# A decoder stack on one core: the order of TensorE's steps in the first cross attention

## The chip, the core and the metric

The kernel runs on one core of a Trainium2 chip. The metric is the device time of one execution in microseconds, in which all six layers of the stack run one after the other.

## What is computed

The reference is two decoder layers on x of 8 batches, 512 tokens and 256 channels. Each layer adds self attention, cross attention over a context of 512 tokens, and a feed forward part. The change touches only the cross attention of the first layer:

```
q = x_q @ W_q;  kv = x_kv @ W_kv;  k, v = kv[..., :C], kv[..., C:]      # 16 heads of 16
q, k = _rotate(q, sin_q, cos_q), _rotate(k, sin_k, cos_k)
att = einsum('bhqd,bhkd->bhqk', q, k) / sqrt(D)
att = where(q_mask & kv_mask, att, -1e9)
y = einsum('bhqk,bhkd->bhqd', softmax(att), v)
x = x + y.reshape(B, T, C) @ W_c
```

## The kernel before

`spread_attention` (L99) does this layer. Its work is cut into steps, and each step has a due time in the table `at` (L114 to L147), in units of one score step. Every engine gets its steps sorted by due time (`in_order`, L165), and runs them in that order, with semaphores between the engines. So the table alone sets the order on TensorE (`pe_steps`), ScalarE (`act_steps`), VectorE (`dve_steps`), GpSimd and the DMA queue of SyncE.

A batch has 32 units, in four groups of eight. A unit u is the score of two heads for 128 rows, and it is computed twice. `max` (L347) scores 128 queries against all keys, and VectorE reduces it to the row maximum (L522). `exact`, due 12.9 units later (L358), scores 128 keys against all queries with the maxima as further rows, and ScalarE takes the exponential (L456). Below, M5 and X5 are the `max` and the `exact` of unit 5. Each is two matmuls on the upper and lower 64 rows of the array at the same time. Both go to one ring of three PSUM slots (`SLOTS`): a score needs the slot of the third score before it, so it waits until VectorE or ScalarE has read that one.

All other steps of TensorE go to two PSUM banks (`BANKS`), and each waits until the bank it takes has been read:

- `value` (L377), 4 per group: exponentials times V, in column tiles of 32.
- `mt` (L364), 1 per group: transposes the maxima, in column tiles of 32. ScalarE (L467) and VectorE (L545) split them, and SyncE's queue moves them into the rows that `exact` reads (L313).
- `qk` (L425), 4 per batch in 2 parts: projections of queries and keys for the next batch. ScalarE copies them (L485).
- `rot` (L433), 4 per batch: the rotation. VectorE multiplies it by the sine (L554), GpSimd makes the rest (`rope`, L617 to L636), and ScalarE rounds the result (`high`, L491).
- `turn` (L385), 4 per batch, and `back` (L391), 2 per batch: transposes of the attention's output.
- `norm` (L410), 2 per batch: transposes of the normalised input, which ScalarE makes in four instructions (`htok`, L473).
- `v` (L441) and `out` (L402), 4 parts of each per batch: the projection of the values and the output projection. VectorE adds the latter to x (L582).

All of these but `value` and `mt` use the full array of 128 x 128. In the steady order of before, nearly every pair X, M is followed by one such step. In all of the stage TensorE goes 580 times from a step of one tile shape to a step of another (counted on the sorted list, 64-row scores, 32-column steps and full steps being the three shapes).

Of the kernel before, what the change touches and what calls it, by code (L numbers as in the profile page):

```python
# [35 lines left out]
KC = C // P  # L36
# [62 lines left out]
def spread_attention(nc, name, x_mem, consts, wq_d, wk_d, wv_d, wo_d, ctx_d, rope, mask_d):  # L99
# [3 lines left out]
    PER_G = UNITS // GROUPS  # L103
# [8 lines left out]
    at = {}  # L112
    for b in range(B):
        o = UNITS * b  # L114
        at[("ctx", b, 0)] = o - 50.0
        for i in range(NT):
            at[("stat", b, i)] = o - 47.4 + i
        at[("root", b, 0)] = o - 42.0
        at[("htok", b, 0)] = o - 40.0
        for c in range(KC):  # L120
            at[("norm", b, c)] = o - 38.0 + c
        for n, t in zip(QK_ORDER, (-44.0, -36.0, -28.0, -20.0)):
            for part in range(KC):
                at[("qk", b, n, part)] = o + t + part + 0.5
            at[("rot", b, n)] = o + t + 2.9
            at[("rope", b, n)] = o + t + 3.0
            at[("high", b, n)] = o + t + 5.6
        for g in range(GROUPS):
            free = o + PER_G * g - 23.8
            for s4 in range(4):  # L130
                at[("stack", b, g, s4)] = free + 0.8 * s4
            at[("mt", b, g)] = o + PER_G * g - 4.1
            at[("mdma", b, g)] = o + PER_G * g - 3.0
            for k in range(NT):
                at[("value", b, g, k)] = o + PER_G * (g + 1) + k - 0.5
            at[("turn", b, g)] = o + PER_G * (g + 1) + 5.2
        for u in range(UNITS):
            at[("max", b, u)] = o + u - LEAD + 0.1
            at[("exact", b, u)] = o + u
        for m, ts in enumerate(((-14.4, -12.8), (1.6, 3.2))):  # L140
            for part, t in enumerate(ts):
                at[("v", b, m, part)] = o + t
        for c, t in enumerate((24.9, 39.2)):
            at[("back", b, c)] = o + t
        for m, ts in enumerate(((41.6, 42.0), (43.2, 43.25))):
            for part, t in enumerate(ts):
                at[("out", b, m, part)] = o + t  # L147

    start = {("root", 0, 0): -31.5, ("htok", 0, 0): -31.1, ("root", 1, 0): -31.0, ("htok", 1, 0): -28.3,
             ("init", 0, 0): -31.4, ("cosine", 0, 0): -29.65,  # L150
# [46 lines left out]
    for n, st in enumerate(pe_steps):  # L197
        if st[0] in ("max", "exact"):
            continue
        if first_part(st) == st:  # L200
            free = [k for k in range(BANKS) if holder[k] is None or done_part(holder[k]) in set(pe_steps[:n])]
            k = min(free, key=lambda k: used[k])
# [34 lines left out]
    for st in pe_steps:  # L237
        if st[0] == "exact":
            pt_slot[st], pt_freed[st] = pt_free.pop(0)
        elif st[0] == "value":  # L240
            _, b, g, k = st
# [2953 lines left out]
def build(nc, a, outs, phases=("band", "cross0", "ffn", "self", "cross1", "moe")):  # L3195

    with ExitStack() as ctx:
# [46 lines left out]
        if "cross0" in phases:  # L3244
            spread_attention(nc, "cross0", x_mem, consts, a["L0_xattn_W_q"], a["L0_xattn_W_k"], a["L0_xattn_W_v"],
                             a["L0_xattn_W_c"], a["ctx_T"], (a["cos0"], a["sin0"], a["turn0"]), a["mask"])
# [136 lines left out]
```

## Times and profile before

| | us |
|---|---|
| median of 3 runs | 3017.0 (3009.43 to 3017.76) |
| span of the profiled execution | 3008.1 |
| first cross attention, from the first score to its last step | 289.4 to 841 |
| TensorE busy over the span | 2752.6 (92%) |
| VectorE, ScalarE, GpSimd busy | 1923.9 (64%), 1450.5 (48%), 1104.9 (37%) |

The stage is about 552 us of the span. TensorE is busy for 510 us of it by the same profile, VectorE 372, ScalarE 342 and GpSimd 144. A busy TensorE in such a view is not one at its peak: matmuls overlap, so what a step costs is read from the start of it to the start of the next.

### The profile page before, as it was taken

The page shows a single profiled execution, that of the slowest core. Times are in us where ns is not written, and L with a number is a line of the kernel's source. Part 1 is how long each engine was busy: PE and PEld are TensorE (multiplying, and loading weights), DVE is VectorE, ACT ScalarE, POOL GpSimd, SP SyncE. Part 2 cuts the span into 40 slices and gives each one's busy share as a digit, 9 for nine tenths or more (in the row PEclk, how much of TensorE's full clock was granted, in tenths as well). Part 3 has the DMA queues.
Part 4 walks back from the last instruction along what each step waited for, and adds up shares of the span by engine and source line. Part 5 has one row for each costly group of instructions (what it writes and reads, how often), then busy time and mean ns, then how long its engine had stood idle before and what let it go on. Part 6 is the DMA issues. An engine that isn't in the chain of part 4 may idle for free. (4 is left out here: it accounts for less than half of the span.)

```text
span 3008.1 us, 49289 instructions
## 1 busy us (share of the span) xinstructions
PE 2752.6 (92%) x16604; PEld 1616.4 (54%) x16605; DVE 1923.9 (64%) x3109; ACT 1450.5 (48%) x2231; POOL 1104.9 (37%) x853
## 2 busy tenths in 40 slices
PE   7997899999868899999999999999889999966998
PEld 4774333333335555555555555555445555556997
DVE  5775776667668766757575757575645555474565
ACT  3342566666668643434343434343335555553333
POOL 3233332222037243434343434443443333153333
PEclk9998899999989999999999999999989999958999
DMA  5002222222111000000000000000043222146665
GB/s 159 0 0 74 54 57 57 55 59 53 34 56 43 1 1 1 0 0 0 0 0 0 0 0 0 0 0 0 1 112 78 72 67 70 45 114 233 216 218 193
DMA packets 102929, 159.71 MB, mean 53 GB/s; under 512 B 28350, under 2 KB 63433, under 8 KB 97161
## 3 DMA queue, kind: packets, MB, share of 16 engines
q1 hardware_dynamic: 97784, 147.88, 17.1%
q0 software_dynamic: 3408, 8.46, 0.8%
q10 hardware_dynamic: 1600, 1.61, 0.2%
q8 instruction: 79, 1.29, 0.2%
q14 instruction: 58, 0.47, 0.1%
HBM read 91.79 MB, written 14.96 MB: 35 GB/s over the span
## 5 line engine op out<-in xcount | busy, mean ns | idle before, releaser
L1672 DVE TENSOR_REDUCE self_nmax<-self_SM 128x2 f32<-128x1024 f32 x256 | 313.9, 1226 | 184.5 <-PE self_SM L1569 177.7
L522 DVE TENSOR_REDUCE cross_nmax<-cross_S 128x2 f32<-128x1024 f32 x256 | 311.9, 1224 | 150.5 <-PE cross_S L347 149.6
L1650 ACT ACTIVATE self_PT<-self_ST 128x1024 f32<-128x1024 f32 x256 | 262.6, 1026 | 292.0 <-PE self_ST L1592 292.0
L1710 POOL TENSOR_TENSOR self_U<-self_PT 128x1024 f32<-128x1024 f32 x64 | 153.0, 2391 | 622.1 <-ACT self_PT L1650 622.1
L1713 POOL TENSOR_TENSOR self_U<-self_U,self_PT 128x1024 f32<-128x1024 f32 x128 | 304.0, 2375 | 55.6 <-ACT self_PT L1650 51.1
L456 ACT ACTIVATE cross_PT<-cross_S 128x1024 f32<-128x1024 f32 x256 | 260.9, 1026 | 114.6 <-PE cross_S L358 113.9
L1186 DVE TENSOR_REDUCE cross_nmax<-cross_S 128x4 f32<-128x1024 f32 x128 | 156.8, 1225 | 143.4 <-PE cross_S L984 143.3
L1602 PE MATMUL self_OP<-self_PT,self_V 128*64 128x512 f32 x1024 | 233.8, 598 | 10.1 <-ACT self_PT L1650 10.1
L1686 DVE RECIPROCAL self_rcp<-self_W 128x512 f32<-128x512 f32 x64 | 214.1, 3345 | 8.4 <-PE self_W L1609 8.4
L1112 ACT ACTIVATE cross_PT<-cross_S 128x1024 f32<-128x1024 f32 x128 | 131.1, 1024 | 119.6 <-PE cross_S L1000 119.6
L1602 PEld LDWEIGHTS self_OP<-self_PT,self_V 128*64 128x64 f32 x1024 | 69.5, 136 | 139.2 <-issue 132.8
L377 PE MATMUL cross_W<-cross_PT,cross_V 128*32 128x512 f32 x1024 | 135.7, 604 | 8.0 <-DVE cross_rsin L554 8.0
L617 POOL TENSOR_TENSOR cross_rows<-cross_rows,cross_cos 128x512 f32<-128x512 f32 x30 | 38.4, 1279 | 276.5 <-DVE cross_rsin L554 276.5
L358 PEld LDWEIGHTS cross_S<-cross_qs,cross_ks 51*128 51x128 f32 x512 | 47.9, 184 | 168.0 <-issue 120.9
L358 PE MATMUL cross_S<-cross_qs,cross_ks 51*128 51x512 f32 x512 | 128.1, 499 | 7.5 <-DVE cross_nmax L522 3.5
L1589 PE MATMUL self_ST<-self_q_hi,self_k_hi 64*128 64x512 f32 x512 | 122.9, 476 | 12.0 <-ACT self_PT L1650 10.8
L1654 ACT COPY self_Oraw<-self_OP 128x512 f32<-128x512 f32 x64 | 37.6, 588 | 197.2 <-PE self_OP L1602 197.2
L1569 PE MATMUL self_SM<-self_k_hi,self_q_hi 64*128 64x512 f32 x512 | 114.2, 441 | 19.1 <-DVE self_nmax L1672 19.1
L347 PE MATMUL cross_S<-cross_ks,cross_qs 49*128 49x512 f32 x512 | 108.6, 421 | 12.6 <-ACT cross_PT L456 11.4
L3103 PE MATMUL moe_TR<-moe_W,moe_hid_hi 128*128 x312 | 114.8, 406 | 0.0
L1617 PE MATMUL self_W<-self_wo,self_OT 128*128 128x256 f32 x512 | 112.5, 380 | 1.0 <-DVE self_OT L1689 1.0
L1689 DVE TENSOR_TENSOR self_OT<-self_Oraw,self_rcp 128x512 f32<-128x512 f32 x64 | 106.9, 1670 | 6.5
(436 smaller groups left out, 6335.7 us busy)
## 6 DMA issues: line engine op xcount, KB each, us to landing
moe_staged<-in_L_ffn_W SPq DMA_DIRECT2D x36, 1024.0 KB
cross_ks<-cross_parts SPq DMA_DIRECT2D x384, 64.0 KB, 2.2
cross_qs<-cross_parts SPq DMA_DIRECT2D x376, 64.0 KB, 2.3
all_x<-in_L_ffn_W SPq DMA_DIRECT2D x14, 1024.0 KB
all_x<-sorted_rows SPq DMA_DIRECT2D x83, 130.0 KB, 2.3
cross_cT<-in_ctx_T SPq DMA_DIRECT2D x16, 512.0 KB, 4.5
sorted_rows<-all_spare_row SPq DMA_DIRECT2D x1, 5460.0 KB, 23.8
all_x<-in_x SPq DMA_DIRECT2D x8, 512.0 KB, 3.7
```

The source lines that it names most:

```text
L358: m = pe.matmul(dst[:, r, :], ks[rows_r, p, k * P:(k + 1) * P], qs[rows_r, p, :], start=True, stop=True)
L377: m = pe.matmul(dst[32 * j:32 * j + 32, :], V[:, b % 2, k, 2 * p + r, :], PT[:, pt_slot[("exact", b, NT * p + k)], r, :], start=(k == 0), ...
L456: act.activation(PT[:, pt_slot[st], :, :], S[:, slot[st], :, :], ACT.Exp).then_inc(s_exped, 1)
L522: dve.tensor_reduce(nmax[:, g % 2, 0:R, n % PER_G], S[:, slot[st], :, :], AX.X, ALU.max, negate=True).then_inc(s_maxed, 1)
L1112: act.activation(PT[:, pt_slot[st], :, :], S[:, slot[st], :, :], ACT.Exp).then_inc(s_exped, 1)
L1186: dve.tensor_reduce(nmax[:, g % 2, 0:R, n0:n0 + 2], S[:, slot[st], :, :].rearrange("p r (i c) -> p r i c", i=2), AX.X, ALU.max, negate=Tru ...
L1602: m = pe.matmul(OP[j * D:(j + 1) * D, :], V[:, k, 2 * n + j, :], PT[:, k, j, :], start=(k == 0), stop=(k == NT - 1), skip_group_check=True)
L1650: act.activation(PT[:, k, :, :], ST[:, :, :], ACT.Exp).then_inc(exped.sem, 1)
L1672: dve.tensor_reduce(nmax[:, i, 0:P:D], SM[:, :, :], AX.X, ALU.max, negate=True).then_inc(maxed.sem, 1)
L1686: dve.reciprocal(rcp[:, :], bank_of(order, st)).then_inc(done, 1)
L1710: pool.tensor_tensor(U[:, c % 2, :, :], PT[:, 0, :, :], PT[:, 1, :, :], ALU.add).then_inc(added.sem, 1)
L1713: pool.tensor_tensor(U[:, c % 2, :, :], U[:, c % 2, :, :], PT[:, k, :, :], ALU.add).then_inc(added.sem, 1)
```

## The change

Only due times change. The diff of `spread_attention`:

```
-        at[("root", b, 0)] = o - 42.0
+        at[("root", b, 0)] = o - 43.0
         at[("htok", b, 0)] = o - 40.0
         for c in range(KC):
-            at[("norm", b, c)] = o - 38.0 + c
+            at[("norm", b, c)] = o - 37.5 + 0.01 * c
         for n, t in zip(QK_ORDER, (-44.0, -36.0, -28.0, -20.0)):
             for part in range(KC):
-                at[("qk", b, n, part)] = o + t + part + 0.5
-            at[("rot", b, n)] = o + t + 2.9
-            at[("rope", b, n)] = o + t + 3.0
-            at[("high", b, n)] = o + t + 5.6
+                at[("qk", b, n, part)] = o + t + 0.05 + 0.01 * part
+            at[("rot", b, n)] = o + t + 1.5
+            at[("rope", b, n)] = o + t + 1.6
+            at[("high", b, n)] = o + t + 4.5
...
-            at[("mt", b, g)] = o + PER_G * g - 4.1
+            at[("mt", b, g)] = o + PER_G * g - 3.96
...
-                at[("value", b, g, k)] = o + PER_G * (g + 1) + k - 0.5
-            at[("turn", b, g)] = o + PER_G * (g + 1) + 5.2
+                at[("value", b, g, k)] = o + PER_G * (g + 1) + (-0.5, 1.05)[k // 2] + 0.01 * (k % 2)
+            at[("turn", b, g)] = o + PER_G * (g + 1) + 5.51
...
-        for m, ts in enumerate(((-14.4, -12.8), (1.6, 3.2))):
-            for part, t in enumerate(ts):
-                at[("v", b, m, part)] = o + t
-        for c, t in enumerate((24.9, 39.2)):
-            at[("back", b, c)] = o + t
-        for m, ts in enumerate(((41.6, 42.0), (43.2, 43.25))):
-            for part, t in enumerate(ts):
-                at[("out", b, m, part)] = o + t
+        for m, t in enumerate((-13.5, 2.5)):
+            for part in range(2):
+                at[("v", b, m, part)] = o + t + 0.01 * part
+        for c in range(KC):
+            at[("back", b, c)] = o + 42.5 + 0.01 * c
+        for m, t in enumerate((50.52, 66.52)):
+            for part in range(2):
+                at[("out", b, m, part)] = o + t + 0.01 * part
```

Sorted, one group of TensorE's steps in the steady state reads like this (u counted within batches 3 and 2, other batches' steps by name):

```
before  X24 M5 value back X25 M6 value X26 norm M7 value X27 norm M8 mt X28 M9 qk X29 M10 turn qk X30 M11 rot X31 M12 value X0 ...
after   X22 M3 X23 M4 | value value | X24 M5 X25 | value value | M6 X26 M7 | norm norm | X27 M8 X28 | mt qk qk | M9 X29 M10 | rot turn | X30 M11 X31 M12 | ...
```

The 16 scores of a group stand in rows of 4, 3, 3, 3 and 3. The block in the place of `norm norm` is, in the four groups of a batch, `norm norm`, `v v out out`, `back back` and `v v out out`. The second `out` pair of a batch moves 23 units later, and `back` moves to one place. TensorE changes tile shape 346 times in place of 580. The other engines keep their steps in nearly the same order: on ScalarE `high` stands right behind the exponential of X0, X8, X16 or X24 (there behind `htok`), and on VectorE the second part of `mt` still stands behind the reduction of M9, M17, M25 or M1. No instruction is added or removed.

## Rows read from the trace of the kernel before

**Rows 1.** Busy time by stretch (busy us and count per engine, clock, DMA share, GB/s): batches 2 and 6

```profile
447.03:514.74 67.71, 64.71 (x364) 25.40 (x360) 47.49 (x59) 43.89 (x58) 19.91 (x19) 1.00 0.23 57
717.90:782.02 64.12, 58.34 (x344) 23.07 (x340) 45.17 (x50) 39.54 (x49) 14.43 (x12) 1.00 0.21 52
```

**Rows 2.** Timeline of TensorE (start, length, what, idle before), batch 2

```profile
477.46 0.50 PE L358 MATMUL cross_S<-cross_qs,cross_ks 51*128 51x512 f32 x2
477.80 0.40 PE L347 MATMUL cross_S<-cross_ks,cross_qs 49*128 49x512 f32 x2
478.13 0.66 PE L385 MATMUL cross_W<-all_ident,cross_Oraw 128*128 128x128 f32 x4
478.62 1.02 PE L425 MATMUL cross_W<-cross_hT,cross_wq 128*128 128x512 f32 x2
479.58 0.51 PE L358 MATMUL cross_S<-cross_qs,cross_ks 51*128 51x512 f32 x2
479.92 0.40 PE L347 MATMUL cross_S<-cross_ks,cross_qs 49*128 49x512 f32 x2
480.43 1.10 PE L433 MATMUL cross_W<-cross_rows,cross_turnm 128*128 128x512 f32 x2
```

**Rows 3.** Timeline of TensorE, batch 2, where it waits

```profile
454.39 0.50 PE L347 MATMUL cross_S<-cross_ks,cross_qs 49*128 49x512 f32 x2 [0.81 <-ACT cross_PT L456]
454.82 1.13 PE L441 MATMUL cross_W<-cross_wv,cross_cT 128*128 128x256 f32 x4
455.88 0.41 PE L364 MATMUL cross_W<-all_ident,cross_nmax 128*32 128x128 f32 x4
456.23 0.51 PE L358 MATMUL cross_S<-cross_qs,cross_ks 51*128 51x512 f32 x2
...
464.59 1.07 PE L377 MATMUL cross_W<-cross_PT,cross_V 128*32 128x512 f32 x8 [1.32 <-DVE cross_rsin L554]
465.59 0.50 PE L358 MATMUL cross_S<-cross_qs,cross_ks 51*128 51x512 f32 x2
```

**Rows 4.** Timeline of TensorE, batch 0: three scores in a row

```profile
313.12 0.51 PE L347 MATMUL cross_S<-cross_ks,cross_qs 49*128 49x512 f32 x2
313.46 0.40 PE L358 MATMUL cross_S<-cross_qs,cross_ks 51*128 51x512 f32 x2
313.69 0.40 PE L347 MATMUL cross_S<-cross_ks,cross_qs 49*128 49x512 f32 x2
```

**Rows 5.** Timeline of TensorE: steps of one shape in a row, prologue and last batch

```profile
280.00 1.88 PE L425 MATMUL cross_W<-cross_cT,cross_wk 128*128 128x512 f32 x4
281.72 1.89 PE L441 MATMUL cross_W<-cross_wv,cross_cT 128*128 128x256 f32 x8
...
831.64 3.64 PE L377 MATMUL cross_W<-cross_PT,cross_V 128*32 128x512 f32 x32
```

**Rows 6.** Timeline of all engines, batch 3: a score and the reduction that reads it

```profile
533.63 0.40 PE L347 MATMUL cross_S<-cross_ks,cross_qs 49*128 49x512 f32 x2
...
534.07 1.23 DVE L522 TENSOR_REDUCE cross_nmax<-cross_S 128x2 f32<-128x1024 f32 x1 [1.83 <-PE cross_S L347]
```

**Rows 7.** Timeline of all engines, batch 2: ScalarE around `htok`

```profile
500.48 2.06 ACT L473 ACTIVATE all_x<-all_x,cross_shift,cross_rstd 128x256 f32<-128x256 f32 x4
...
502.91 1.02 ACT L456 ACTIVATE cross_PT<-cross_S 128x1024 f32<-128x1024 f32 x1
```

**Rows 8.** Timeline of all engines, batch 7: from the maxima to the score that reads them

```profile
792.07 0.33 DVE L545 SCALAR_TENSOR_TENSOR cross_mrow<-cross_mhi,cross_lows,cross_W 64x128 fp32r<-64x128 f32 x1
...
796.43 0.50 PE L358 MATMUL cross_S<-cross_qs,cross_ks 51*128 51x512 f32 x2
```

**Rows 9.** Groups of instructions, batch 2: VectorE and ScalarE (busy, mean ns, idle before)

```profile
L554 DVE TENSOR_TENSOR cross_rsin<-cross_W,cross_sin 128x512 f32<-128x512 f32 x4 | 2.7, 681 | 0.0
L491 ACT CAST cross_parts<-cross_rows 128x512 fp32r<-128x512 f32 x4 | 2.5, 616 | 4.2 <-POOL cross_rows L629 4.2
```

**Rows 10.** Costliest groups of the page: GpSimd's first step of the rotation

```profile
L617 POOL TENSOR_TENSOR cross_rows<-cross_rows,cross_cos 128x512 f32<-128x512 f32 x30 | 38.4, 1279 | 276.5 <-DVE cross_rsin L554 276.5
```

## The prediction

> **What bounds the kernel now.** I read the busy times by stretch first. A middle batch of this stage takes 67.7 us, and TensorE is busy for 64.7 of it at full clock, VectorE for 47.5, ScalarE for 43.9 and GpSimd for 19.9 [rows 1]. The other middle batches show the same pattern of starts, so one batch can be priced for all. Then I read TensorE's timeline of batch 2, from start to start, which shows two things. The first is idle time with a releaser, 3.5 us per batch: 0.8 to 1.0 us where M16 waits for a slot of the ring that ScalarE reads, 1.3 to 1.4 us where a `value` waits for its bank, which VectorE still reads for the sine product [rows 3], and three waits under 0.3. The second is a cost at each change of tile shape that no wait shows. Two scores, from the first's start to the start of another shape, take 0.67 us (477.46 to 478.13 [rows 2]), while a score between two scores takes 0.23 (313.46 to 313.69 [rows 4]). So two scores among scores would be 0.46, and entering and leaving such a pair costs 0.21. A `value` between scores takes 1.00 (464.59 to 465.59 [rows 3]); four in a row take 3.64 to the end of the last, whose own length is 1.06 to 1.07 [rows 3, 5], so (3.64 - 1.06) / 3 = 0.86 each. A `v` part on its own takes 1.06 (454.82 to 455.88 [rows 3]), and a part of `qk` in a row 1.72 / 2 = 0.86 (280.00 to 281.72 [rows 5]). One change of shape therefore costs 0.1 on the side of the scores and 0.05 to 0.1 on the side of the other step.
>
> The page on TensorEngine tiling of the Trainium skill ("TensorEngine Tiling (Array Packing)", Key Properties) says that a change of tiling mode drains the engine. The rows just named agree, at 0.1 to 0.2 us for each change.
>
> **The change, part by part.** No instruction is added, so the sum is the price of every row and block of the new order, plus the waits that this order makes.
>
> TensorE's own time in one batch, without waits:
> - 16 rows of three scores at 0.67 + 0.23 = 0.90, and 4 rows of four at 1.13: 18.9 us [rows 2, 4].
> - 8 pairs of `value`: 0.86 + 1.00 = 1.86 each, 14.9 us [rows 3, 5].
> - 4 blocks `mt qk qk`: `mt` takes 0.35 (455.88 to 456.23 [rows 3]), entering the full shape 0.10, then 0.86 and, as behind `turn` now, 0.96 (478.62 to 479.58 [rows 2]): 2.27 each, 9.1 us. `mt` directly ahead of `qk` is in no row; 0.10 is between nothing and the 0.2 of a whole change.
> - 4 blocks `rot turn`: 0.96 as for a lone `qk` part behind its like, and `turn` 0.49 (478.13 to 478.62 [rows 2]) plus 0.05 for leaving: 1.5 each, 6.0 us. Today `rot` starts 0.51 us after its M (479.92 to 480.43), where `turn` starts 0.33 after its own [rows 2]: it waits for ScalarE's copy of `qk`. Now a row of three lies between, which at 0.90 us covers the 0.6 us copy, so 4 x 0.18 us go.
> - `norm norm` and `back back` at twice a `turn` plus leaving, 1.03 each, and two blocks `v v out out` at 0.96 + 0.86 + 0.86 + 0.96 = 3.64 each: 9.3 us.
>
> The sum is 58.2 us. The same prices for the order of before give 64.3 us, and 64.3 + 3.5 of waits is 67.8 against the measured 67.7 [rows 1], so the prices hold. Without waits the new order would save 9.5 us per batch.
>
> The waits of the new order come from the ring of three slots. A score behind a score is read 0.44 us after its start (533.63 to 534.07 [rows 6]), one behind another shape 0.10 later, as its successor starts 0.34 after it in place of 0.23 [rows 4]. The reading takes 1.02 on ScalarE and 1.23 on VectorE [rows 6, 7], and TensorE goes on some 0.06 later. I walk through one group, with c as the start of its row of four (X30 M11 X31 M12):
> - M12 takes X30's slot. X30 is read from c + 0.54 to c + 1.56, so M12 starts at c + 1.64 at the earliest, where it could at c + 0.81. That is 0.83 us, in every group: 3.3 per batch.
> - VectorE at that point has M9, the second part of `mt`, M10, the sine product (0.68 us [rows 9]) and `turn` before it, and reaches M11 at about c + 2.2 and M12 at c + 3.4, done at c + 4.65. X1, third in the next row, needs M12's slot and could start at c + 4.4. That is 0.3 us, four times: 1.2 per batch.
> - `htok` holds ScalarE for 2.06 us between X24 and X25 [rows 7]. Today it costs next to nothing, since M7, which takes X25's slot, starts only then (502.91 + 1.02 against M7 at 503.99 [rows 7]). In the new order X25 directly follows M5, and `high` (0.62 us [rows 9]) stands ahead of its exponential too: that ends about 5.25 us after X24's start, and M7 could have started at 3.6. That is 1.7 us, once per batch.
> - M23, last in its row, is read second of two. X12 takes its slot, and between them lies only `back back`: 0.45 us, once. Behind `norm norm` `qk` waits 0.25 for ScalarE's copy of the second `norm`.
> - What the maxima need is nearly a tie. From the end of VectorE's part to the score that reads the rows are 796.43 - 792.40 = 4.03 us [rows 8], where the score waited for the transfer. In the new order VectorE's part ends about 5.3 us after X27's start, and X0 is due 9.4 + 0.8 after it. I take no wait; a later VectorE would make one.
>
> These are 6.9 us, so a batch takes 58.2 + 6.9 = 65.1, which is 2.6 less than now. The two waits that rows 3 show go: `value` no longer follows `back` at once, and M16 stands a row later.
>
> Over the stage: five full batches (1 to 5) give 13. The second half of batch 0 gives 1. Batch 6, which has no projections to make in its last two groups [rows 1], takes 64.1 now, of which over 8 are waits of the same ring and of the maxima; I take 4. In batch 7 `out` and `back` of the last batches move to the end, where nothing covers them (two parts of `out` at 0.86, a `back` and its copy, about 1 us each), which takes what its rows win: 0. The start, up to X0 of batch 0, waits on transfers and on GpSimd, and I take 0. The sum is 18 us. The profiled execution would go from 3008.1 to 2990, and the median, taken as 8.9 us above it again, from 3017 to 2999.
>
> **The rivals.**
> A. The ring hardly waits, since VectorE and ScalarE have 20 us spare in each batch [rows 1], and the rows and blocks are long enough. For it: the averages. Against it: M12 cannot start before X30 is read, whatever the average. With waits of 1.5 us a batch takes 59.7, and 6.5 batches save 8 each: 3017 - 50 = 2967. Chance 0.15.
> B. The forecast, 2999, with 2985 to 3008 as its own range. Chance 0.48.
> C. The readers take all of it back. VectorE's queue runs in order, with the second part of `mt` and `turn` between reductions, and each M X M row puts 2.5 us of reductions on it at once. If the third score of half of the rows waits 0.5 us more than above, 10 x 0.25 to 10 x 0.5 are 2.5 to 5 us and the saving is gone: 3008 to 3020, at 3015. Chance 0.22. The same page of the Trainium skill (PSUM Bottleneck) warns that tiling speeds TensorE but not the reading of PSUM, which may then bind; no row of before shows the ring at that density.
> D. Slower, by one mechanism: `high`. It stands in ScalarE's queue right behind X0's exponential, and waits for GpSimd, whose two or three steps of 1.28 us each [rows 10] start at the sine product. Already ScalarE idles 4.2 us per batch ahead of it [rows 9]. By my walk the last step ends at about c + 5.65 for the queries, and X0 has been read at c + 5.4, which costs 0.25 us and is covered. From c + 6.1 on, X1's exponential, queued behind, holds up M15, and every microsecond is one of TensorE's, four times per batch. At c + 7.4 that is 4 x 1.3 = 5.2 us per batch, 2.6 more than the change saves: 3017 + 6.5 x 2.6 = 3034. It decides from c + 6.75. Chance 0.15, some of it for a start that is later by some microseconds.
>
> **How the numbers follow.** The likeliest is B, 2999. The range takes B whole, most of C and most of A, 2972 to 3018. A measurement of this kernel can tell about 0.3%, 9 us, from no change, so faster means below 3008. A, nearly all of B and little of C make 0.68 faster; the rest of B, most of C and a little of D 0.2 the same; D and a bit of C 0.12 slower.
>
> **What would show it right or wrong.** In the changed kernel's timeline a row of three should take 0.90 us and a pair of `value` 1.86. M4, M12, M20 and M28 should each show an idle time of 0.6 to 0.9 us on ScalarE's exponential. M7 should idle 1.5 to 2 us on the same line, and X1, X9, X17 and X25 about 0.3 on VectorE's reduction. From X0 to X0 of the next batch should be 65.1 us. If that is 60 the waits were too many in my walk (A), if 67 VectorE's queue is longer (C), and if ScalarE's idle time ahead of L491 is over 8 us per batch it is D. It would be wrong altogether if a middle score cost more than 0.23 us in the steady state, or if the clock fell in this stage, which is at full level in every middle batch now [rows 1].

## The result and the profile after

The changed kernel takes 3024.2 us (median of 17 runs, 3020.6 to 3031.9) and the kernel before 3013.6 (17 runs). The ratio is 1.0034, with a 95% interval of 1.0027 to 1.0040. The prediction of 2999, range 2972 to 3018, was wrong: the time lies above the range, and it moved the other way. The profiled execution has a span of 3026.5 us, 18.3 more than that of before. By the starts of X0 in the two timelines, batches 1 to 5 take 353.1 us in place of 338.7 (14.3 more) and the time up to X0 of batch 1 grew by 7.1. Batch 6 grew by 0.1, batch 7 lost 2.1, and what follows the stage lost 1.1. The forecast started from 3017, the median of the three runs known then; from 3013.6 its saving of 18 us would be 2996, so the starting point did not cause the miss.

The busy times by stretch of the changed kernel, one row for each of batches 3, 4 and 5 (stretch, length, busy us and count of PE, PEld, DVE, ACT and POOL, granted clock, DMA share, GB/s), answer to [rows 1]:

```profile
528.40:598.71 70.31, 61.52 (x364) 28.88 (x360) 47.41 (x58) 43.45 (x58) 19.88 (x20) 0.98 0.22 55
598.71:667.51 68.80, 59.94 (x364) 27.97 (x360) 47.32 (x58) 43.11 (x58) 19.89 (x20) 1.00 0.22 56
667.51:739.31 71.80, 63.13 (x365) 29.18 (x362) 47.31 (x58) 43.22 (x58) 19.89 (x20) 0.95 0.22 53
```

TensorE is busy for 59.9 us of a batch at full clock, where it was busy for 64.7 [rows 1]. So the work did become denser, and still the batch is longer: TensorE idles 8.9 us of it in place of 3.0. Batches also differ now, with the granted clock. Batch 4, at 1.00, is the one to price.

Who TensorE waited for, in most of the stage (345 to 800 us), in the changed kernel (waiting line, releaser, us in total, times, longest):

```profile
PE cross_W L433 <- DVE cross_mrow L545: 27.3, 25, 1.1
PE cross_S L347 <- ACT cross_PT L456: 26.0, 33, 1.5
PE cross_S L358 <- DVE cross_nmax L522: 3.6, 9, 0.8
```

The second and third row are the ring, which was foreseen. The first row was not: `rot` waits for VectorE's part of `mt`, L545, 1.1 us each time by the profile (1.17 from start to start, below). The timeline of all engines around `rot` in batch 4 shows how (start, length, what, idle before):

```profile
606.91 0.41 PE L364 MATMUL cross_W<-all_ident,cross_nmax 128*32 128x128 f32 x4
...
607.26 1.98 PE L425 MATMUL cross_W<-cross_cT,cross_wk 128*128 128x512 f32 x4
...
608.39 0.25 ACT L467 CAST cross_mhi<-cross_W 64x128 fp32r<-64x128 f32 x1
...
609.28 0.60 ACT L485 ACTIVATE cross_rows<-cross_W 128x512 f32<-128x512 f32 x1 [0.64 <-PE cross_W L425]
...
609.71 1.23 DVE L522 TENSOR_REDUCE cross_nmax<-cross_S 128x2 f32<-128x1024 f32 x1 [1.62 <-PE cross_S L347]
609.74 0.39 PE L347 MATMUL cross_S<-cross_ks,cross_qs 49*128 49x512 f32 x2
...
610.85 0.33 DVE L545 SCALAR_TENSOR_TENSOR cross_mrow<-cross_mhi,cross_lows,cross_W 64x128 fp32r<-64x128 f32 x1
...
611.24 1.12 PE L433 MATMUL cross_W<-cross_rows,cross_turnm 128*128 128x512 f32 x2 [1.11 <-DVE cross_mrow L545]
```

`rot` takes the PSUM bank that `mt` used. ScalarE has rounded the maxima by 608.64, and VectorE is idle until 609.71 (its reduction shows 1.62 us of idle time). But the reduction of M17 stands ahead of L545 in VectorE's order, and M17 comes only behind `mt qk qk`. So L545 starts at 610.85 and frees the bank at 611.18, when TensorE has had nothing to do since M18. From the start of M18 to that of `rot` are 1.50 us, where 0.33 is the price without a wait: 1.17 us, four times per batch. ScalarE's copy of `qk` (L485) was done at 609.88 and is not what was waited for.

The clock is the second surprise. In batch 2 it went down just behind the pause ahead of M7:

```profile
505.00:512.00 7.00, 5.99 (x46) 1.81 (x44) 4.37 (x5) 5.03 (x8) 2.31 (x2) 1.00 0.26 62
512.00:514.00 2.00, 0.83 (x6) 0.59 (x7) 0.98 (x2) 2.00 (x4) 1.27 (x1) 1.00 0.39 93
514.00:516.00 2.00, 2.00 (x11) 1.57 (x11) 0.93 (x1) 1.66 (x4) 0.00 (x0) 0.52 0.38 93
516.00:518.00 2.00, 2.00 (x9) 0.69 (x8) 1.23 (x1) 1.99 (x3) 0.00 (x0) 0.50 0.06 15
518.00:520.00 2.00, 2.00 (x4) 0.67 (x2) 0.00 (x0) 0.00 (x0) 0.00 (x0) 0.50 0.02 4
```

and M7 and the two `qk` parts behind it, by the timeline of TensorE:

```profile
513.17 0.50 PE L347 MATMUL cross_S<-cross_ks,cross_qs 49*128 49x512 f32 x2 [1.52 <-ACT cross_PT L456]
...
517.23 3.78 PE L425 MATMUL cross_W<-cross_hT,cross_wq 128*128 128x512 f32 x4
```

The granted clock falls from 1.00 to 0.50 (2.4 to 1.2 GHz) behind a stretch in which TensorE was busy for 0.83 of 2 us. The `qk` parts take 3.78 us, against 1.98 in batch 4 (607.26 above). Such a fall comes right behind M7 in batches 1, 2, 3 and 5, 24 us at half clock by the clock's own records, and none in batch 4. Before, these batches had none. The five batches take 70.6 us on average, 1.8 more than batch 4, and the difference between batches 2 (71.95) and 4 (68.80) is 3.15. Batch 6 has 10 us at half clock, where it had none before.

### The profile page after: what moved, and what is told of

The parts are those of the page before. It is cut to its first block and busy times, and to the rows that moved or that the text cites. A ratio compares the mean times of both kernels' runs of the same rounds, so it can differ in the third digit from the quotient of the medians.

```text
span 3026.5 us, 49289 instructions
## 1 busy us (share of the span) xinstructions
PE 2736.6 (90%) x16604; PEld 1644.9 (54%) x16605; DVE 1924.5 (64%) x3109; ACT 1444.7 (48%) x2231; POOL 1102.8 (36%) x853
## 3 DMA queue, kind: packets, MB, share of 16 engines
q10 hardware_dynamic: 1600, 1.61, 0.2%
## 5 line engine op out<-in xcount | busy, mean ns | idle before, releaser
L347 PE MATMUL cross_S<-cross_ks,cross_qs 49*128 49x512 f32 x512 | 117.5, 459 | 28.5 <-ACT cross_PT L456 27.6
L358 PE MATMUL cross_S<-cross_qs,cross_ks 51*128 51x512 f32 x512 | 118.1, 460 | 12.2 <-DVE cross_nmax L522 6.5
L377 PE MATMUL cross_W<-cross_PT,cross_V 128*32 128x512 f32 x1024 | 124.6, 605 | 0.0
L1589 PEld LDWEIGHTS self_ST<-self_q_hi,self_k_hi 64*128 64x128 f32 x512 | 47.8, 183 | 114.3 <-ACT self_PT L1650 62.8
```

The lines of the kernel that those rows point to most:

```text
L1589: pe.matmul(ST[:, j, :], l[at, slot, at_k], r[at, slot, :], start=(t == 0), stop=False)
```

## The experiments

Times are medians, ratios are against runs of the kernel before on the same chip. Its median goes from 3013.6 to 3019.2 us from chip to chip, so two experiments from different chips are better compared by their ratios. The first four experiments ran on one chip, the next four on a second, and the last two on a third. "Per batch" is from X0 to X0, batches 2 to 5, unless one is named.

**The part of `mt` on VectorE ahead of one reduction.**

```
-    dve_steps = ... lambda st: soon(st, 0.3) if st[0] in dve_kinds else at[st]
+    lag = {"mt": 0.03}; dve_steps = ... lambda st: soon(st, lag.get(st[0], 0.3)) if ...
```

> The changed kernel, with VectorE's part of mt ahead of the reduction of M9, M17, M25, M1 in its queue; TensorE's order is the same. Theory 1 (rot waits for its bank, which VectorE's part of mt frees only behind that reduction): rot follows its row at once, 4 x 1.17 = 4.7 us per batch go, a batch at full clock takes 68.8 - 4.7 = 64.1 us, the whole 3024 - 6.5 x 4.7 = 2994. Theory 2 (rot waits for ScalarE's copy of qk): rot starts as late as before, 3024. If the pause of 1.7 us ahead of M7 is what brings the clock down, stretches at half clock remain in some of the batches 1 to 5 (24 us of them in the changed kernel).

Measured: 2996.7 us, ratio 0.9941 (0.9924 to 0.9958). The same steps in batch 4 now, all engines, and behind them TensorE's timeline of M18 and `rot`:

```profile
579.12 0.41 PE L364 MATMUL cross_W<-all_ident,cross_nmax 128*32 128x128 f32 x4
...
580.58 0.25 ACT L467 CAST cross_mhi<-cross_W 64x128 fp32r<-64x128 f32 x1
580.87 0.34 DVE L545 SCALAR_TENSOR_TENSOR cross_mrow<-cross_mhi,cross_lows,cross_W 64x128 fp32r<-64x128 f32 x1 [0.58 <-ACT cross_mhi L467]
...
581.93 1.23 DVE L522 TENSOR_REDUCE cross_nmax<-cross_S 128x2 f32<-128x1024 f32 x1 [0.72 <-PE cross_S L347]
```

```profile
581.96 0.40 PE L347 MATMUL cross_S<-cross_ks,cross_qs 49*128 49x512 f32 x2
582.29 1.12 PE L433 MATMUL cross_W<-cross_rows,cross_turnm 128*128 128x512 f32 x2
```

L545 starts 1.75 us behind `mt` and no longer 3.94, in time in which VectorE is idle, and delays no reduction. From M18 to `rot` are 0.33 us, and the wait for L545 is gone from the list of waits. A batch takes 64.4 to 64.5 us (expected 64.1; 66.0 in batch 5, which has a stretch at half clock), 4.3 less than batch 4 had at full clock; 0.2 of what is missing is a new wait of M15. One edit of VectorE's order, with TensorE's order unchanged, is worth 0.9% of the kernel and turns the change from a loss into a gain. Of the 31 us by which batches 1 to 5 are shorter, 23 are the waits of `rot` themselves (20 x 1.17), and most of the rest is time at half clock that goes with them. Theory 1 holds, and theory 2 falls. In this profiled execution 3.4 us at half clock are left in batches 1 to 5, although the pause ahead of M7 is as long as before (1.90 us from X26 to M7, of which 0.23 is the price of the score).

**`htok` earlier.**

```
-        at[("htok", b, 0)] = o - 40.0
+        at[("htok", b, 0)] = o - 40.5
```

> The changed kernel with htok due half a unit earlier, ahead of X24's exponential in ScalarE's queue and not behind it. The wait of M7 falls from 1.7 us to about 0.3. If this pause is what brings the clock down, no stretch at half clock is left in batches 1 to 5 and a batch takes 68.8 - 1.4 = 67.4, so 5 x (70.6 - 67.4) = 16 us less, 3008. If it is the sum of all waits of the stage, half-clock stretches remain, and only 5 x 1.4 = 7 us go, 3017.

Measured: 3011.7 us, ratio 0.9987 (0.9977 to 0.9997). From X26 to M7 are 0.24 us, so the wait is all gone and not only most of it. No half clock is left in batches 1 to 5, and a batch takes 67.6 us (expected 67.4), while the `rot` waits are still there at 27.5 us in 25 times. So in these profiled executions the pause of 1.7 us with the four waits of 0.8 (the experiment above) hardly brings the clock down, the four waits of 1.17 with the four of 0.8 do not at all, and all of them together do in four batches of five. The expectation took the pause for the cause; by these profiles neither kind of wait does it alone. Each of these is one execution. The mean granted clock of the executions goes down to 0.962 with `mt` early and to 0.963 with `htok` early, where the profiled ones have 0.965 (the changed kernel: 0.962 to 0.966, profiled 0.963). That is up to 18 and 12 us more at half clock somewhere in the kernel, and where is not on record.

**Both.**

> Both edits. Theory 1 with the pause as the cause of the clock's fall: 64.1 - 1.4 = 62.7 us per batch, all at full clock; against the changed kernel 7.9 less in five batches and 4 less in one or two others, 3024 - 45 = 2979, and 1% under the kernel before. Under theory 2: as with htok alone.

Measured: 2986.9 us, ratio 0.9911 (0.9894 to 0.9928). A batch takes 63.2 us (expected 62.7), all of batches 1 to 6 at full clock:

```profile
502.69:565.89 63.20, 60.32 (x364) 27.93 (x360) 46.69 (x59) 43.25 (x58) 19.92 (x19) 1.00 0.24 61
```

What is left of waits in a batch is 0.81 four times for the row of four, 0.47 twice where X12 and X28 wait for VectorE, and 0.2 at M15. Against the changed kernel the median is 37 us less, where 45 was expected, and the span of the profiled execution is 45.4 less (2981.1 against 3026.5). The executions of both kernels spread by about 10 us, so the two agree no better than that. By the profiled executions, the 27.1 us against the kernel before are 24.5 in batches 1 to 5, 4.1 in batch 6 and 1.1 up to batch 1, while batch 7 takes 3.1 more, with stretches at half clock that were not taken apart further.

**Control: VectorE's part of `mt` earlier in the kernel before.** The edit of the first experiment, on the old due times.

> Control: the kernel before with VectorE's part of mt ahead of the reduction of M9 and its like. There turn takes the bank of mt, two rows later, and waits 0.1 us for it. If the edit helps only by the changed order's rot, this is 3013 within 3 us. If an earlier transfer of the maxima were worth something by itself, it would be 3005 or less.

Measured: 3013.8 us, ratio 0.9995 (0.9984 to 1.0005). A batch takes 67.6 in place of 67.7. The earlier transfer of the maxima is worth nothing by itself. In this kernel the step matters only where a bank is taken from `mt` early. It is not quite free: batches 6 and 7 of this profile have 14 us at half clock, where the kernel before has none, and take 4.3 us more. Batch 7 is longer with this edit in all three pairs of profiles: 63.4 against 60.7 us here, 64.2 against 58.6 in the changed kernel, and 63.7 against 59.6 with `htok` early.

**`turn` apart from `rot`.**

```
-            at[("turn", b, g)] = o + PER_G * (g + 1) + 5.51
+            at[("turn", b, g)] = o + PER_G * (g + 1) + 6.5
```

on top of both edits.

> Both edits of e3_both and turn due one unit later, between M11 and X31: the row of four, X30 M11 X31 M12, becomes two pairs with turn between them. If M12's wait of 0.81 us is X30's reading, it is now covered by turn, for one more visit of the full shape at 0.34 us: 63.2 - 4 x 0.47 = 61.3 us per batch and 2987 - 12 = 2975 in all. If the wait comes back at another score of the ring, it stays 2987.

Measured: 2983.7 us, ratio 0.9891 (0.9873 to 0.9909), beside 0.9911 of the kernel with both edits. TensorE's timeline of batch 3:

```profile
510.11 1.13 PE L433 MATMUL cross_W<-cross_rows,cross_turnm 128*128 128x512 f32 x2
511.17 0.50 PE L358 MATMUL cross_S<-cross_qs,cross_ks 51*128 51x512 f32 x2
511.50 0.39 PE L347 MATMUL cross_S<-cross_ks,cross_qs 49*128 49x512 f32 x2
511.82 0.66 PE L385 MATMUL cross_W<-all_ident,cross_Oraw 128*128 128x128 f32 x4
512.41 0.50 PE L358 MATMUL cross_S<-cross_qs,cross_ks 51*128 51x512 f32 x2
512.78 0.50 PE L347 MATMUL cross_S<-cross_ks,cross_qs 49*128 49x512 f32 x2
```

The fourth score starts 1.61 us after the first, as it did in the row of four (1.62), but now `turn` stands in between. A batch takes 62.2 us, 1.0 less where 1.9 was expected: M15 waits 0.54 us for ScalarE in place of 0.2, and the other 0.6 us were not taken apart. In all only 3 us are gained (6 by the ratios), within the intervals. In this run's profile batch 6 has a granted clock of 0.89 and takes 64.4 us, where it had 1.00 and took 60.0 with the row of four, so the last batches gave back what the middle ones won.

**`value` in single steps again**, on top of both edits.

```
-   at[("value", b, g, k)] = o + PER_G * (g + 1) + (-0.5, 1.05)[k // 2] + 0.01 * (k % 2)
+   at[("value", b, g, k)] = o + PER_G * (g + 1) + k - 0.5
```

> Both edits of e3_both, but the four value steps of a group one unit apart again, as in the kernel before. TensorE changes shape 449 times in place of 346. At 0.17 us for a change that is 103 x 0.17 = 17 us more, 3004. If pairs of value gain nothing because the scores' readers need that time anyway, 2987 to 2990.

Measured: 3004.9 us, ratio 0.9954 (0.9937 to 0.9971). That is 18 us above the kernel with both edits, for 103 more changes of tile shape, 0.17 us each. But the two ran on different chips, and by the ratios it is 13 us or 0.13 each (0.06 to 0.20 by the intervals). The trace of a batch is the closer measure: it takes 65.6 in place of 63.2, which is 2.4 us for 13 more changes, 0.18 each. Its waits are as long in sum as with the pairs (M15 and M6 wait 0.9 us more, the second `norm` 0.3 more, X12 and X28 0.9 less). The cost of a change of shape is real in the whole time, and pairs of `value` pay, once the waits are not in the way.

**The suspected wait doubled.** VectorE's part of `mt` with a lag of 1.1 in the changed kernel: behind the reduction of M10 as well.

> The changed kernel with VectorE's part of mt one reduction later still, behind that of M10, M18, M26 and M2: the suspected wait doubled. Theory 1: rot waits 1.2 us more, 2.4 in all, 4 x 1.2 x 6.5 = 31 us more than 3024, 3055, and some more if the maxima's transfer then reaches X0, X8, X16 and X24 late. Theory 2, under which rot does not wait for that part: 3024.

Measured: 3097.8 us, ratio 1.0256 (1.0232 to 1.0279). TensorE in batch 3:

```profile
590.43 0.40 PE L347 MATMUL cross_S<-cross_ks,cross_qs 49*128 49x512 f32 x2
593.06 1.12 PE L433 MATMUL cross_W<-cross_rows,cross_turnm 128*128 128x512 f32 x2 [2.23 <-DVE cross_mrow L545]
```

From M10 to `rot` are 2.63 us in place of 1.50, 1.13 more, as expected. But the kernel lost 74 us (67 by the ratios) and not 31. The rest is the clock. In batches 1 to 5 there are 99 us at half clock, where the changed kernel had 24, and a batch takes 81.9 us at a granted clock of 0.87:

```profile
560.91:642.82 81.91, 69.15 (x364) 31.51 (x361) 47.95 (x58) 43.21 (x58) 19.85 (x19) 0.87 0.19 46
```

68.8 + 4 x 1.13 = 73.3 would be the time at full clock, and 8.6 us per batch come on top, from about 20 us at half clock per batch.

**One part alone: `value` in pairs in the kernel before.** The reverse of the edit to `value` above, on the old due times.

> One part of the change alone: the kernel before with the four value steps of a group in two pairs, all else as it was. TensorE changes shape 485 times in place of 580: 95 x 0.17 = 16 us less than 3014, 2998. If waits of the ring and the banks take it back, 3008 or more.

Measured: 3026.2 us, ratio 1.0030 (1.0016 to 1.0045), a batch 68.7 in place of 67.7. TensorE in batch 3:

```profile
522.52 0.40 PE L347 MATMUL cross_S<-cross_ks,cross_qs 49*128 49x512 f32 x2
522.76 0.40 PE L358 MATMUL cross_S<-cross_qs,cross_ks 51*128 51x512 f32 x2
524.43 0.51 PE L347 MATMUL cross_S<-cross_ks,cross_qs 49*128 49x512 f32 x2 [1.27 <-ACT cross_PT L456]
```

There are 95 changes of shape fewer, 12 per batch or 2.0 us, and against them new waits, most of them of the ring: M16 waits 1.4 us (1.0 before), M24 and M0 0.9 each (0.3 for M0 before), M8 0.6, and the steps around it 0.1 to 0.2 each. These are 3.0 us more per batch, so a batch is 1.0 longer, 5 us in batches 1 to 5. Batch 6 takes 72.1 in place of 64.1, with 20 us at half clock. So this part of the change is by itself a loss of the same size as the whole, by the ring and the clock: `rot` stands in its old place, and no wait for L545 shows. The expectation of 2998 was wrong. Pairs of `value` are a gain in one order (the experiment on single steps above) and a loss in the other. What in the new order makes the difference was not separated; here most of the new waits are of scores for a slot that ScalarE or VectorE still reads.

**`high` one unit later**, with `turn` apart and with the row of four.

```
-            at[("high", b, n)] = o + t + 4.5
+            at[("high", b, n)] = o + t + 5.5
```

> The three edits of e5_turn_apart and high due one unit later, behind X1, X9, X17 and X25 in ScalarE's queue (two of them behind the copy of value as well). In e5_turn_apart M15 waits 0.54 us once per batch for X1's exponential, which stands behind a high that GpSimd ends late. Without it a batch takes 62.2 - 0.5 = 61.7 us and the whole 2984 - 4 = 2980. If high is then late for the rope or the transfers of queries and keys, new waits show at M0, M8 or M16, and the time is 2984 or more.

> e3_both, with high due one unit later as well; the row of four stays. M15's wait there is 0.2 us per batch, so 63.2 - 0.2 = 63.0, and 2986 in all, 1 us from e3_both. Against e9_high_late it gives the worth of the row of four again, with more rounds: 1.3 us per batch in batches 1 to 5, and less or nothing in all if batches 6 and 7 lose to the clock in the one what the others win.

Measured: 2982.3 us with `turn` apart, ratio 0.9885 (0.9862 to 0.9909), and 2985.2 with the row of four, ratio 0.9895 (0.9872 to 0.9918). A batch takes 61.6 and 62.9 us. M15's wait is gone in both, which shows that the early `high`, which waited for GpSimd, was its cause. The row of four costs 1.3 us per batch, and again the two do not differ in the whole beyond the intervals. Batches 6 and 7 of both have stretches at half clock. The kernel with all four edits is the best one found, 1.15% under the kernel before and, by the ratios, 1.5% under the changed one.

## Why the prediction was wrong

**The prices of rows and blocks** were right. The sum was 58.2 us per batch. Batch 4 takes 68.80, and without its waits (4.7 of `rot`, 4 x 0.82, 1.68 and 0.46) 58.7; the 0.5 us are about 0.1 for each score that had to wait, whose successor starts that much later. A row of three takes 0.88 us and a pair of `value` 1.85. The experiment that undoes the pairs of `value` confirms the cost of a change of shape, 0.18 us by the batch. The 9.5 us that the prediction says the order would save without waits set the new order without waits against the old one with them. Like for like its prices gave 64.3 - 58.2 = 6.1 us per batch.

**The ring's waits** were nearly right. M12's wait was put at 0.83 and is 0.82, M7's at 1.7 and is 1.68, X12's at 0.45 and is 0.46. X1's 0.3 us, four times, and the 0.25 of `qk` are not there in batch 4, so 6.9 us should have been 5.4.

**The step that failed** is the one on `rot turn`, together with the list of waits, in which a wait of `rot` for its bank has no term. The prediction asked what `rot` reads, found ScalarE's copy of `qk`, and took 0.18 us of waiting off. It did not ask which PSUM bank `rot` takes and who empties it. In the old order `turn` takes the bank of `mt`, two pieces behind it, and `rot` that of `turn`. In the new one `rot` takes the bank of `mt`. The walk even had L545 behind M9's reduction in VectorE's queue, and used it for M11, M12 and the transfer of the maxima, but not for the bank that L545 frees. This term is 4 x 1.17 = 4.7 us per batch. Put in, the sum would have been 58.2 + 6.9 + 4.7 = 69.8 against 67.7 before: slower by 2.1 us in each of 6.5 batches, 14 us, where 11 were measured. So this term alone puts the sum on the right side. That its size also comes out is in part luck: the ring's waits in it are 1.5 us too long, the clock's cost is missing, and the two cancel. Outside batches 1 to 5 the forecast was 12 us too low as well, of which batch 7 and what follows the stage gave back 3. Up to X0 of batch 1 it had 1 us less and there were 7.1 more, 4.0 of them in batch 0, which has the four waits of `rot` and the pause ahead of M7 too. In batch 6 it had 4 less and there was 0.1 more, with two waits of `rot` and 10 us at half clock.

**The clock** was named among what would make it wrong, with no chance of its own. Measured against batch 4 it costs 1.8 us per batch in batches 1 to 5, 9 us in all. Batch 1, though, is 1.7 us shorter than the others where all are at full clock (65.84 against 67.57 us with `htok` early), so the clock's cost is nearer 11 us of the 18.3 between the two profiled executions. At full clock throughout these batches would take about 342 us, 3.5 more than before: by this estimate the change would have lost time in these batches without the clock too, and in this profile the clock made most of the loss. It comes from idle time that the new order makes, as two experiments show, with one profile each: each takes one kind of wait away, and the clock stays up (or nearly so). The Trainium skill ("TensorE: Matmul & The Clock Gate", "A second HAM failure mode: psum-queue depth-cycling") tells of a kernel whose short idle times between groups, as it cycles through PSUM, make the clock go up and down. The traces here agree: no wait in the changed kernel's middle batches is over 1.7 us.

**The rivals.** C had the right direction, VectorE's order, and the wrong place, a score in the ring in place of a bank. D, `high`, did not happen in the changed kernel: ScalarE idles 0.0 us ahead of L491 in batch 4, where over 8 was D's sign. It shows once `mt` is early, and is small: M15's 0.2 us, and 0.5 with `turn` apart. A is out, as the ring's waits are 5.4 us per batch and not 1.5.

**What stays open.** How the clock decides is not settled. With `mt` early the pause ahead of M7 stands in every batch and the clock falls in one of five, and that is one execution. Nor is it settled why batch 7 takes 3 us more in the kernel with both edits, beyond that VectorE's earlier `mt` lengthens it. Of the 7 us that the changed kernel needs more up to batch 1, 3.1 lie ahead of X0 of batch 0, 1.8 of them ahead of the stage; with the old order and `mt` early X0 comes 4.0 later than in the kernel before, so this part need not be the new order's.

## What to carry to other kernels

When steps are put into another order, write down for each moved step every buffer that it takes, who empties it, and what stands ahead of that reader in its own queue. Data that a step reads is only half of what it waits for. Then move the reader along with the step: here one place in VectorE's order was the difference between 0.3% slower and 0.6% faster. And where the order makes the work denser, look for a single pause that is longer than the others, since here several short ones and one longer one together took the clock down, and then they cost more than their length.

## What the runs showed of the hardware

The clock went to half level in batches 1, 2, 3 and 5 of the changed kernel, though TensorE was busy for 61.5 of 70.3 us (batch 3) and no wait was over 1.7 us. Doubling four waits of 1.17 us per batch raised the time at half clock from 24 to 99 us in five batches. A batch took 81.9 us in place of 70.6 for 4.5 us more of waits, so the added waits cost 2.5 times their own length. Taking either kind of wait away (those of 1.17 us, or the one of 1.7) brought the time at half clock to 3.4 us or none, in one profiled execution each.

A change of tile shape between 64-row scores and 32-column steps cost 0.18 us, by 2.4 us for 13 more changes in a batch at full clock.
